# Row one-hots of a graph attention pass moved from VectorE to ScalarE, with the weights' copy and the first gathers re-ordered

## Chip, cores, metric

One core of a Trainium2 chip. The metric is the device time of one execution in microseconds; lower is better. PE is TensorE, DVE VectorE, ACT ScalarE, POOL GpSimd, SP the engine that issues most DMAs.

## What is computed

The reference is one layer of a graph network on 6250 nodes of 256 features and 100,000 edges sorted by destination. Three branches act on the normalised nodes, and the part that matters here is the first:

```python
q = (x @ Wq + bq).reshape(N, H, C)          # H = 4 heads, C = 64
k = (x @ Wk + bk).reshape(N, H, C)
v = (x @ Wv + bv).reshape(N, H, C)
alpha = jnp.sum(q[dst] * k[src], axis=-1) / jnp.sqrt(C)
amax = jax.ops.segment_max(alpha, dst, num_segments=N)
a = jnp.exp(alpha - amax[dst])
denom = jax.ops.segment_sum(a, dst, num_segments=N) + 1e-16
wv = jax.ops.segment_sum(a[:, :, None] * v[src], dst, num_segments=N)
out = wv / denom[:, :, None]
```

The second branch is linear attention with a dense block of two layers (768 hidden, gelu). A mixture of eight experts of three 256x256 layers follows on the sum.

## The kernel before

The kernel has three long stages: preparation and projections (to about 470 us), the edge pass with the dense block woven into it (to about 1860 us), and the experts.

**The edge pass.** Edges are laid out in 208 half groups (`NHF`) of four slots (`HG`) of 128 edges, each slot belonging to one window of 128 nodes. All engines run the same sequence of steps i = 0, 1, ..., each in its own instruction order, tied by semaphores; `c` is i modulo 24.

- POOL gathers the k and v rows of a half group with four indirect DMAs into one of 12 places of `ring` (`gather`, L777). From half group 12 on it waits until the place is free.
- SP loads the edges' row numbers, broadcast to all partitions, into one of four `relq` tiles (`relq_load`, L487), four half groups ahead, once `ohT_made` says that the tile was used.
- DVE makes the row one-hots `ohT` of half group i+1 (`row_one_hots`, L1652), multiplies k by the spread q (`products`, L1658), sums into `alpha` (`scores`, L1664), in `weigh` (L1711) scales v of half group i-7 (`LAG` is 7) by its attention weights, and in `add_up` (L1725, or L1720 to L1723) adds bank 0 of half group i-8 to its nodes.
- PE spreads q to edges with the one-hots (`spread_q` of half group i+2, L1210; one PSUM tile, so it needs `prod_made` of i+1), and sums v into nodes (`gather_up` of i-7, L1221), which counts `agg_ps`. Before `gather_up` PE waits for `acc_made` and `acc_copied` of i-8.
- ACT makes the one-hots for the sums in place of k (`sum_keys` of i-7: four Abs L876 and a Relu L879) and copies the other three banks of half group i-8 to the nodes (`new_windows`, L885, when `agg_ps` allows).

Every fourth step belongs to a chunk of four half groups (`CH`): a maximum over segments in steps with c % 4 = 0 (DVE L1674, L1675, then PE L1250), carries in steps with c % 4 = 1 (DVE L1681 to L1693, then PE L1256), differences with c % 4 = 2 (DVE L1699 to L1702, exponentials on ACT L905 and L907, then PE L1262 and L1263), and with c % 4 = 3 ACT copies the weights from PSUM into the ring (L898, counts `a_made`).

**The dense block** runs beside it, in turns of eight steps: `dense(c, m)` gives a turn g (0 to 24, 256 nodes in each) and a phase p = (c - 3) % 8. PE's part of a phase comes first in its step, DVE's and ACT's last. Phase 0 is the product with `w_qf` (L1166) and the start of a layer norm (DVE L1621 to L1629, ACT's square root L858), phase 1 its end (DVE), phase 2 a transpose (PE L1172, ACT L862), phases 3 to 5 the first dense layer (PE L1181, two gelus each on ACT, L868), phases 4 to 7 the second (PE L1188), and phase 7 the next turn's transpose (L1155, L853). PE's phase 4 begins with the first layer's second third, which re-uses the PSUM bank of the first:

```python
                if p in FC1:
                    pe.wait_ge(sem("fc_in"), 32)
                    pe.wait_ge(sem("m_hT_sb"), g + 1)
                    if p > 3:
                        pe.wait_ge(sem("gelu"), g * NM + 2 * (p - 3))
```

So steps with c % 4 = 2 are those of phases 3 and 7, and c % 4 = 0 those of phases 1 and 5.

## Time and profile before

| | |
|---|---|
| runs of the kernel | median 2830.92 us of 3 (2825.30 to 2831.41) |
| the profiled execution | 2825.32 us, its span 2823.6 us |
| busy share of the span | PE 89%, PE's weight loads 77%, DVE 79%, ACT 54%, POOL 33% |
| from 1000 to 1100 us, a stretch of the edge pass | PE 89.39, DVE 92.03, ACT 60.50, POOL 65.33 us busy; granted TensorE clock 0.98; DMA share 0.67 |
| chain that ended last | PE 55%, DVE 18%, issue 6%, ACT 2% |

The span is what the profile covers; the 1.7 us around it belong to the execution. The share of busy time is an average, so the stretch of the edge pass is read by itself. In rows of waits and timelines, `<-` names what ended an engine's idle time.

### The profile page before, as it was taken

The numbers are of one execution on the slowest core, as the hardware profiler recorded it, in microseconds if no ns is written. First come the engines' busy times: TensorE is split into PE (matmuls) and PEld (weight loads), VectorE is DVE, ScalarE is ACT, GpSimd is POOL, SyncE is SP. The second block draws the span as 40 slices with busy tenths as digits, with TensorE's granted clock in tenths as the row PEclk, the third lists the DMA queues.
The fourth block names the chain that finished last, engine by engine and source line by source line (L and its number), as shares of the span: only waits on it lengthen the run. The fifth ranks groups of instructions, "written<-read, shape, count | busy, mean of one in ns | idle before, by whom it ended". The sixth has DMA issues, their size and how long they took to land.

```text
span 2823.6 us, 50437 instructions
## 1 busy us (share of the span) xinstructions
PE 2508.7 (89%) x15651; PEld 2177.1 (77%) x15651; DVE 2236.2 (79%) x4398; ACT 1532.6 (54%) x3157; POOL 939.5 (33%) x891
## 2 busy tenths in 40 slices
PE   4388996899898898998998998759999999999999
PEld 2266774677777777777776776549999999999998
DVE  8797554899999999999999999756677777666775
ACT  0411110465665656655665656556666666666665
POOL 0330003666666666666666666300000000000000
PEclk9699998899999999999999999869999999999999
DMA  5210445766666666666666666510000000000000
GB/s 166 79 46 21 147 137 186 214 201 202 199 196 204 195 200 205 193 198 201 200 198 195 204 202 196 153 43 16 11 11 15 15 15 15 15 15 11 11 14 10
DMA packets 189958, 335.56 MB, mean 119 GB/s; under 512 B 31456, under 2 KB 129008, under 8 KB 189766
## 3 DMA queue, kind: packets, MB, share of 16 engines
q0 software_dynamic: 67104, 219.09, 25.9%
q1 hardware_dynamic: 116378, 108.11, 12.6%
q10 hardware_dynamic: 6316, 6.40, 0.8%
q8 instruction: 80, 1.31, 0.2%
q14 instruction: 80, 0.66, 0.1%
HBM read 293.81 MB, written 40.48 MB: 118 GB/s over the span
## 4 chain that ended last, share of the span: by engine, by line
PE 55%; DVE 18%; issue 6%; ACT 2%; DVEq 1%; DMA 1%; ACTq 0%; SPq 0%
PE ps L1324 16%; PE ps L1221 9%; PE ps L1210 8%; PE ps L1334 8%; PE ps L1188 4%; DVE ring L1658 3%; PE ps L1181 3%; DVE ring L1711 2%; PE ps L1166 2%; ACT f_more L953 1%; DVE f_split L1842 1%; DVE nodes L1725 1%; PE ps L1306 1%; DMA relq<-rel_rows 1%; DVE f_more L1858 1%
## 5 line engine op out<-in xcount | busy, mean ns | idle before, releaser
L777 POOL DMA_INDIRECT ring<-kv_rows,idx x832 | 887.4, 1067 | 738.9 <-DMA idx<-src_cols 294.8
L1324 PE MATMUL ps<-f_split,e_up 128*128 128x256 f32 (+1 forms) x3200 | 595.6, 286 | 3.5 <-DVEq L1872 1.3
L953 ACT ACTIVATE f_more<-ps,e_rest 128x256 f32<-128x256 f32 (+1 forms) x800 | 402.2, 553 | 277.7 <-PE ps L1324 276.6
L1324 PEld LDWEIGHTS ps<-f_split,e_up 128*128 128x128 f32 x3200 | 498.3, 192 | 17.4 <-issue 8.0
L1210 PE MATMUL ps<-nodes,ohT 128*128 x1664 | 413.8, 393 | 63.2 <-DVE ring L1658 56.9
L1842 DVE TENSOR_TENSOR f_split<-f_more,f_split 128x512 fp32r<-128x512 f32 (+1 forms) x400 | 272.8, 682 | 229.0 <-ACT f_split L958 222.1
L1324 PE MATMUL ps<-f_split,e_low 128*128 128x256 f32 (+1 forms) x1600 | 453.0, 283 | 0.0
L1221 PE MATMUL ps<-ring 128*128 128x260 f32 x1664 | 447.3, 415 | 0.0
L1210 PEld LDWEIGHTS ps<-nodes,ohT 128*128 128x128 f32 x1664 | 319.8, 196 | 133.0 <-issue 86.9
L1221 PEld LDWEIGHTS ps<-ring 128*128 128x128 f32 x1664 | 317.7, 201 | 43.6
L885 ACT ACTIVATE nodes<-ps 128x780 f32 x208 | 170.9, 822 | 270.3 <-PE ps L1221 249.8
L1324 PEld LDWEIGHTS ps<-f_split,e_low 128*128 128x128 f32 x1600 | 307.2, 192 | 0.0
L1334 PE MATMUL ps<-e_up,f_split 128*128 128x256 f32 x1568 | 291.3, 283 | 0.9 <-DVE f_split L1842 0.9
L876 ACT ACTIVATE ring<-iota_f,relC 128x128 f32<-128x128 f32 x832 | 263.8, 392 | 0.0
L1664 DVE TENSOR_REDUCE alpha<-ring 128x16 f32<-128x1024 f32 x208 | 254.0, 1221 | 7.1
L1711 DVE TENSOR_TENSOR ring<-ring 128x1024 f32<-128x1024 f32 x208 | 252.4, 1213 | 8.6 <-ACT ring L898 8.5
L1658 DVE TENSOR_TENSOR ring<-ring,ps 128x1024 f32<-128x1024 f32 x208 | 252.4, 1214 | 7.3 <-PE ps L1210 5.7
L1334 PEld LDWEIGHTS ps<-e_up,f_split 128*128 128x128 f32 x1568 | 244.5, 192 | 1.1 <-DVE f_split L1842 1.1
L1334 PE MATMUL ps<-e_low,f_split 128*128 128x256 f32 x784 | 221.6, 283 | 0.0
L1410 DVE TENSOR_TENSOR rows<-work,rows 128x1024 bf16<-128x1024 bf16 x196 | 159.6, 889 | 18.8 <-PE ps L1006 17.6
L1858 DVE SCALAR_TENSOR_TENSOR f_more<-ps,small,f_more 128x256 f32<-128x256 f32 x392 | 170.9, 477 | 0.7 <-PE ps L1334 0.7
L1334 PEld LDWEIGHTS ps<-e_low,f_split 128*128 128x128 f32 x784 | 150.5, 192 | 0.0
(314 smaller groups left out, 3556.2 us busy)
## 6 DMA issues: line engine op xcount, KB each, us to landing
relq<-rel_rows SPq DMA_DIRECT2D x208, 128.0 KB, 4.2
ring<-kv_rows,idx POOLq DMA_INDIRECT x832, 4.3
kv_rows<-work SPq DMA_DIRECT2D x49, 256.0 KB, 2.0
xn_rows<-nodes SPq DMA_DIRECT2D x1, 6272.0 KB, 20.4
sx_rows<-work SPq DMA_DIRECT2D x49, 128.0 KB, 1.8
nodes<-in_x_dram ACTq DMA_DIRECT2D x4, 1536.0 KB
work<-in_x_dram SPq DMA_DIRECT2D x48, 128.0 KB, 2.1
m_xn<-xn_rows SPq DMA_DIRECT2D x24, 256.0 KB, 4.3
```

The source lines that it names most:

```text
L777: pool.indirect_dma_start(out=kvh(c)[:, g, 0:2 * D], out_offset=None, in_=kvD, in_offset=bass.IndirectOffsetOnAxis(ap=idx[c // KP][:, s:s ...
L876: ins = act.activation(kv[:, g, 0:P], iota_f[:, :], ACT.Abs, bias=relC[:, ds(j * HG + g, 1)], scale=-1.0)
L953: ins = act.activation(f_whole[l][:, m * T2 * P:m * T2 * P + n * P], bank(2 * l + e % 2, m * T2 * P, m * T2 * P + n * P), ACT.Relu, bias=e ...
L1210: last = pe.matmul(ps[:, 2048 + D * g:2048 + D * (g + 1)], ohT[c % 2][:, g * P:(g + 1) * P], nodes[:, ds(win[g] * AC + HG * AC, D)], start ...
L1221: last = pe.matmul(to, kvh(cj)[:, g, 0:P], kvh(cj)[:, g, D:SL], start=(g == 0), stop=False, skip_group_check=True)
L1324: last = pe.matmul(bank(2 * l + e % 2, m * T2 * P, m * T2 * P + n * P), e_parts[l][w][:, e, i, m * P:(m + 1) * P], src_[a][:, i * T2 * P:i ...
L1334: last = pe.matmul(bank(4 + e % 2, t * D, (t + 1) * D), f_h[1][e % 2][a][:, i * T2 * P + t * P:i * T2 * P + (t + 1) * P], e_parts[2][w][:, ...
L1658: dve.tensor_tensor(k, k, ps[:, 2048:3072].rearrange("p (g d) -> p g d", g=HG), ALU.mult).then_inc(sem("prod_made"), 1)
L1664: dve.tensor_reduce(alpha[c // CH % 2][:, :].rearrange("p (h s) -> p s h", h=H)[:, c % CH * HG:(c % CH + 1) * HG, :], kvh(c)[:, :, 0:D].re ...
L1711: dve.tensor_tensor(v4, v4, kv[:, :, 2 * D:SL].unsqueeze(3).broadcast_to([P, HG, H, C]), ALU.mult).then_inc(sem("oh2_made"), 1)
L1842: dve.tensor_tensor(lo, whole, up.bitcast(F32), ALU.subtract).then_inc(sem(("h1_lo", "h2_lo")[l]), 1)
L1858: ins = dve.scalar_tensor_tensor(out=yt, in0=bank(4 + e % 2, t * D, (t + 1) * D), scalar=f_w[b][:, t * NE + e:t * NE + e + 1], in1=yt, op0 ...
```

## The change

1. The row one-hots leave DVE. ACT makes them two half groups ahead, as an Abs of (row number's difference to the partition) and a Relu of one minus it, into one of three `ohT` tiles in place of two. SP loads the first four `relq` tiles earlier, ahead of the projections' stores.
2. In ACT's step the order changes: `new_windows` and the exponentials come first, then the row one-hots, then `sum_keys`, now of half group i-6 (it waits for `alpha_made`), then, at the end of the chunk's third step (c % 4 = 2) in place of the next step, the copy of the chunk's weights, then the dense phase.
3. POOL's gathers of half groups 5 to 11 wait for the products of the half group four earlier.

```diff
--- before.py
+++ after.py
@@ -68,6 +68,7 @@
     CS = CH * HG
     NCH = NHF // CH
     LAG = 7
+    AHEAD = 4
     SHIFT = 3
     U = 2 * KP
     TURNS = NHF // U
@@ -215,7 +216,7 @@
         pen = [mid(f"pen{b}", [CS * H, P + 8], F32) for b in range(2)]
         mid("gap3", [P, AN - 2 * MH - MH // P * D - 4 * W4 - NM * TG * P - 2 * (KP * HG + CS * H + P + 8)], F32)
         ring = mid("ring", [P, RING], F32)
-        ohT = [mid(f"ohT{b}", [P, HG * P], F32) for b in range(2)]
+        ohT = [mid(f"ohT{b}", [P, HG * P], F32) for b in range(3)]
         relq = [mid(f"relq{b}", [P, HG * P], BF16) for b in range(4)]
         segF = mid("segF", [CS * H, P], F32)
         segB = mid("segB", [CS * H, P], F32)
@@ -460,6 +461,12 @@
             sp.wait_ge(sem("rows_out"), 48)
             sp.wait_ge(sem("pen_out"), 16)
 
+            def relq_load(i, c):
+                sp.dma_start(relq[c % 4][:, :], relD[ds(i * HG, HG), :].rearrange("(a g) e -> a (g e)", a=1).partition_broadcast(P)).then_inc(sem(f"relq_in{c % 4}"), 16)
+            sp.wait_ge(sem("tables_made"), 6)
+            for i in range(4):
+                relq_load(i, i)
+
             sp.sem_inc(sem("stored"), CREDIT)
 
             def store(t, k):
@@ -483,9 +490,6 @@
                 sp.dma_start(a_row[NF * i:NF * i + n, :], w.rearrange("(k p) -> k p", p=P)).then_inc(sem("mix_in"), 16)
 
 
-            def relq_load(i, c):
-                sp.dma_start(relq[c % 4][:, :], relD[ds(i * HG, HG), :].rearrange("(a g) e -> a (g e)", a=1).partition_broadcast(P)).then_inc(sem(f"relq_in{c % 4}"), 16)
-
             def chunk_load(k, b):
                 for h in range(H):
                     sp.dma_start(pen[b][h * CS:(h + 1) * CS, 0:P + 1], penD[ds(k * CS, CS), :]).then_inc(sem(f"chunk_in{b}"), 16)
@@ -510,8 +514,6 @@
             idx_load(0, 0)
             idx_load(1, 1)
             sp.wait_ge(sem("att_sb"), 8)
-            for i in range(4):
-                relq_load(i, i)
             mix_load(m_xn, xnD, 0, TG, "m_xn_in")
             mix_load(m_sx, sxD, 0, TG, "m_sx_in")
             sp.dma_start(w_f1[:, :, :], w_fc1.rearrange("(k p) n -> p k n", p=P)).then_inc(sem("fc_in"), 16)
@@ -771,6 +773,8 @@
                     pool.wait_ge(sem("att_sb"), 8)
                 if not isinstance(i, int) or i >= KP:
                     pool.wait_ge(sem("agg_ps"), i - (KP - 1))
+                elif i > AHEAD:
+                    pool.wait_ge(sem("prod_made"), i - AHEAD)
                 pool.sem_inc(sem("begun"), 1)
                 for g in range(HG):
                     s = c % KP * HG + g
@@ -872,12 +876,22 @@
 
             def sum_keys(j, cj):
                 kv = kvh(cj)
+                act.wait_ge(sem("alpha_made"), j + 1)
                 for g in range(HG):
                     ins = act.activation(kv[:, g, 0:P], iota_f[:, :], ACT.Abs, bias=relC[:, ds(j * HG + g, 1)], scale=-1.0)
                 ins.then_inc(sem("far_made"), 1)
                 act.wait_ge(sem("far_made"), j + 1)
                 act.activation(kv[:, :, 0:P], kv[:, :, 0:P], ACT.Relu, bias=1.0, scale=-1.0).then_inc(sem("sum_keys"), 1)
 
+            def row_one_hots(i):
+                t = ohT[i % 3][:, :]
+                act.wait_ge(sem(f"relq_in{i % 4}"), i // 4 * 16 + 16)
+                if i >= 3:
+                    act.wait_ge(sem("qg_ps"), i - 2)
+                act.activation(t, relq[i % 4][:, :], ACT.Abs, bias=iota_p[:, 0:1], scale=-1.0).then_inc(sem("rows_far"), 1)
+                act.wait_ge(sem("rows_far"), i + 1)
+                act.activation(t, t, ACT.Relu, bias=1.0, scale=-1.0).then_inc(sem("ohT_made"), 1)
+
             def new_windows(j):
 
                 _, base = nc.values_load_multi_w_load_instructions(base_w[0:1, ds(j, 1)], engines=(act.engine,), min_val=0, max_val=NW - 1)
@@ -887,16 +901,6 @@
 
             def step(i, c, m):
                 known = isinstance(i, int)
-                if not known or 0 <= i - LAG < NHF:
-                    sum_keys(i - LAG, (c - LAG) % U)
-                if c % CH == 3 and (not known or i >= 7 and i - 7 < NHF):
-                    kk = m * (U // CH) + (c - 7) // CH
-                    act.wait_ge(sem("ex_T"), kk + 1)
-                    if not known or i > LAG:
-                        act.wait_ge(sem("agg_ps"), i - LAG)
-                    s0 = (c - 7) % KP * HG
-                    act.activation(ring[:, s0 * SL:(s0 + CS) * SL].rearrange("p (s a) -> p s a", a=SL)[:, :, 2 * D:SL],
-                                   PS_EX.rearrange("p (h s) -> p s h", h=H), ACT.Copy).then_inc(sem("a_made"), 1)
                 if not known or i >= LAG + 1:
                     new_windows(i - (LAG + 1))
                 if c % CH == 2 and (not known or i >= 6 and i - 6 < NHF):
@@ -905,12 +909,26 @@
                     act.activation(open_m[:, 0:H], open_m[:, 0:H], ACT.Exp).then_inc(sem("open_ex"), 1)
                     act.wait_ge(sem("diff_made"), kk + 1)
                     act.activation(segD[:, :], segD[:, :], ACT.Exp).then_inc(sem("ex_made"), 1)
+                if i + 2 < NHF:
+                    row_one_hots(i + 2)
+                if 0 <= i - (LAG - 1) < NHF:
+                    sum_keys(i - (LAG - 1), (c - LAG + 1) % U)
+                if c % CH == 2 and (not known or i >= 6 and i - 6 < NHF):
+                    kk = m * (U // CH) + (c - 6) // CH
+                    act.wait_ge(sem("ex_T"), kk + 1)
+                    if not known or i >= LAG:
+                        act.wait_ge(sem("agg_ps"), i + 1 - LAG)
+                    s0 = (c - 6) % KP * HG
+                    act.activation(ring[:, s0 * SL:(s0 + CS) * SL].rearrange("p (s a) -> p s a", a=SL)[:, :, 2 * D:SL],
+                                   PS_EX.rearrange("p (h s) -> p s h", h=H), ACT.Copy).then_inc(sem("a_made"), 1)
                 g, p = dense(c, m)
                 if not known or 0 <= g < NG:
                     mix(g, p, TG, 1 if known and g == NG - 1 else TG)
                 elif g == NG:
                     mix(g, p, 1, 0)
             act.wait_ge(sem("acc_zero"), 1)
+            for i in range(2):
+                row_one_hots(i)
             mix_turned(0, TG)
             for i in range(LAST):
                 step(i, i % U, i // U)
@@ -1207,7 +1225,7 @@
                 if not isinstance(i, int) or i >= 1:
                     pe.wait_ge(sem("prod_made"), i)
                 for g in range(HG):
-                    last = pe.matmul(ps[:, 2048 + D * g:2048 + D * (g + 1)], ohT[c % 2][:, g * P:(g + 1) * P], nodes[:, ds(win[g] * AC + HG * AC, D)], start=True, stop=True)
+                    last = pe.matmul(ps[:, 2048 + D * g:2048 + D * (g + 1)], ohT[i % 3][:, g * P:(g + 1) * P], nodes[:, ds(win[g] * AC + HG * AC, D)], start=True, stop=True)
                 last.then_inc(sem("qg_ps"), 1)
 
             def gather_up(j, cj, place, width):
@@ -1645,12 +1663,6 @@
                 dve.wait_ge(sem("fc2_ps"), g + 1)
                 dve.tensor_tensor(m_sx[:, 0:n * D], bank(7, 0, n * D), m_sx[:, 0:n * D], ALU.add).then_inc(sem("m_out"), 1)
 
-            def row_one_hots(i, c, m):
-                dve.wait_ge(sem(f"relq_in{c % 4}"), m * (U // 4 * 16) + (c // 4 * 16 + 16))
-                if not isinstance(i, int) or i >= 2:
-                    dve.wait_ge(sem("qg_ps"), i - 1)
-                dve.tensor_scalar(ohT[c % 2][:, :], relq[c % 4][:, :], iota_p[:, 0:1], None, ALU.is_equal).then_inc(sem("ohT_made"), 1)
-
             def products(i, c, m):
                 dve.wait_ge(sem(f"kv_in{c % KP}"), kv_seen(c, m))
                 dve.wait_ge(sem("qg_ps"), i + 1)
@@ -1727,8 +1739,6 @@
             def step(i, c, m):
                 known = isinstance(i, int)
                 k = lambda d: m * (U // CH) + (c - d) // CH
-                if not known or i + 1 < NHF:
-                    row_one_hots(i + 1, (c + 1) % U, m + (c + 1) // U)
                 if not known or i < NHF:
                     products(i, c, m)
                     scores(i, c, k(0))
@@ -1759,7 +1769,6 @@
                 elif g == NG:
                     mix(g, p, 1)
             dve.wait_ge(sem("acc_zero"), 4)
-            row_one_hots(0, 0, 0)
             for i in range(LAST):
                 step(i, i % U, i // U)
             dve.wait_ge(sem("acc_made"), NHF)
```

## Rows read from the trace of the kernel before

**Rows 1.** Page, part 5: costliest groups, the gathers.
```profile
L777 POOL DMA_INDIRECT ring<-kv_rows,idx x832 | 887.4, 1067 | 738.9 <-DMA idx<-src_cols 294.8
```

**Rows 2.** Windows: start:end, length, busy us of PE, PEld, DVE, ACT, POOL, granted clock, DMA share, GB/s.
```profile
1040.90:1068.00 27.10, 27.10 (x144) 22.92 (x143) 23.98 (x42) 15.94 (x34) 18.36 (x18) 1.00 0.67 194
1023.80:1027.70 3.90, 3.84 (x16) 3.03 (x17) 3.87 (x6) 0.00 (x0) 0.01 (x1) 0.57 0.52 165
```

**Rows 3.** Waits from 800 to 1600 us: total, times, longest.
```profile
PE ps L1210 <- DVE ring L1658: 28.8, 16, 1.8
```

**Rows 4.** Timeline, PE, in two turns: start, length.
```profile
1010.33 2.00 PE L1221 MATMUL ps<-ring 128*128 128x260 f32 x8
...
1019.61 1.99 PE L1210 MATMUL ps<-nodes,ohT 128*128 x8 [1.80 <-DVE ring L1658]
1023.86 0.37 PE L1250 MATMUL ps<-ident,segF 64*1 64x64 f32 x2 [2.26 <-DVE segB L1675]
...
1024.48 3.33 PE L1221 MATMUL ps<-ring 128*128 128x260 f32 x8
...
1030.21 0.36 PE L1256 MATMUL ps<-ones_row,row_box 1*64 1x1 f32 x4 [0.23 <-DVE row_box L1687]
...
1036.64 0.35 PE L1262 MATMUL ps<-row_box,ones_row 1*128 1x4 f32 x2 [0.34 <-DVE nodes L1725]
...
1037.22 2.00 PE L1221 MATMUL ps<-ring 128*128 128x260 f32 x8
...
1040.91 1.89 PE L1181 MATMUL ps<-m_T,w_f 128*128 128x256 f32 x8
...
1071.83 1.99 PE L1210 MATMUL ps<-nodes,ohT 128*128 x8 [1.80 <-DVE ring L1658]
...
1092.88 1.89 PE L1181 MATMUL ps<-m_T,w_f 128*128 128x256 f32 x8
```

**Rows 5.** Timeline, DVE, in the first of them.
```profile
1015.82 0.69 DVE L1621 TENSOR_TENSOR m_x<-ps,b_qf 128x512 f32<-128x512 f32 x1 [1.23 <-PE ps L1166]
...
1018.14 1.21 DVE L1658 TENSOR_TENSOR ring<-ring,ps 128x1024 f32<-128x1024 f32 x1
...
1024.35 0.48 DVE L1652 TENSOR_SCALAR ohT<-relq,iota_p 128x512 f32<-128x512 bf16 x1
1024.75 1.21 DVE L1658 TENSOR_TENSOR ring<-ring,ps 128x1024 f32<-128x1024 f32 x1
...
1030.37 0.70 DVE L1652 TENSOR_SCALAR ohT<-relq,iota_p 128x512 f32<-128x512 bf16 x1
1031.10 1.22 DVE L1658 TENSOR_TENSOR ring<-ring,ps 128x1024 f32<-128x1024 f32 x1
```

**Rows 6.** Timeline, ACT, in the same turn.
```profile
1012.43 0.22 ACT L898 ACTIVATE ring<-ps 128x64 f32<-128x64 f32 x1 [0.17 <-PE ps L1221]
...
1033.72 1.28 ACT L905 ACT_TABLE_LOAD   x1
...
1035.43 1.28 ACT L868 ACT_TABLE_LOAD   x1
1036.73 0.84 ACT L868 ACTIVATE m_gT<-ps,m_col 128x256 f32<-128x256 f32 x2
```

**Rows 7.** Groups by form, DVE, from 474 to 1862 us.
```profile
L1652 DVE TENSOR_SCALAR ohT<-relq,iota_p 128x512 f32<-128x512 bf16 x208 | 102.2, 491 | 9.5 <-DMA relq<-rel_rows 7.7
```

**Rows 8.** Groups by form, ACT, from 474 to 1862 us.
```profile
L876 ACT ACTIVATE ring<-iota_f,relC 128x128 f32<-128x128 f32 x832 | 263.8, 392 | 0.0
...
L879 ACT ACTIVATE ring<-ring 128x512 f32<-128x512 f32 x208 | 131.3, 631 | 6.6
```

**Rows 9.** Timeline, DVE, start of the edge pass.
```profile
490.59 0.53 DVE L1652 TENSOR_SCALAR ohT<-relq,iota_p 128x512 f32<-128x512 bf16 x1 [2.88 <-DMA relq<-rel_rows]
```

**Rows 10.** Timeline, POOL, start of the edge pass.
```profile
482.88 0.95 POOL L777 DMA_INDIRECT ring<-kv_rows,idx  x1 [0.31 <-issue]
```

**Rows 11.** DMA issues, 440 to 520 us, the gathers.
```profile
ring<-kv_rows,idx POOLq DMA_INDIRECT x44, 4.7
```

## Prediction

> **What bounds the kernel now.** I began with the busy shares. In the edge pass DVE is busy for 92 us in 100 and PE for 89, ACT for 61. That invites the sum "208 one-hots off DVE", so I asked next who waits for whom. PE's longest waits on DVE come once in a turn of eight steps: 16 waits of 1.8 us in 800 us [rows 3]. I therefore laid one whole turn out in time. PE waits 1.80 us for `products` of the phase 1 step, 2.26 us for its segment maximum, 0.23 us for the carries of phase 2 and 0.34 us for `add_up` of phase 3 [rows 4]. From then on PE is busy for 27.10 of 27.10 us at full clock [rows 2]: phases 4 to 7 and 0 are bound by PE, phases 1 to 3 by DVE. The turn repeats after 1071.83 - 1019.61 = 52.2 us [rows 4]. So the change is to be priced along this alternating path, not by DVE's share.
>
> I measure from T, the start of `products` in the phase 1 step (1018.14 [rows 5]). Marks on the path are: the sums' matmuls of phase 3 at 1037.22, T + 19.08, and the start of phase 4 on PE at 1040.91, T + 22.77 [rows 4]. The next turn has T = 1070.36 (its spread starts 1.47 us behind T, as here) and phase 4 at 1092.88, T + 22.52 [rows 4].
>
> **DVE's part, phases 1 to 3.** A one-hot takes 491 ns [rows 7], but overlaps what follows: 0.40 us from its start to that of `products` in one step (1024.35 to 1024.75), 0.73 in a slow one (1030.37 to 1031.10) [rows 5]. The maximum of phase 1 stands behind no one-hot of its own step, so its sums stay at T + 6.34 (1024.48 [rows 4]). Without the one-hot `products` of phase 2 starts at T + 6.21. PE's carry matmuls came 5.46 us behind `products` (1030.21 - 1024.75 [rows 4, 5]), so now at T + 11.67. `Products` of phase 3 comes 5.62 us behind those of phase 2 (1030.37 - 1024.75), at T + 11.83, and PE's L1262 5.54 behind that (1036.64 - 1031.10), at T + 17.37; the sums 0.58 later at T + 17.95. PE itself gets there at about the same time. That is 1.13 us earlier than T + 19.08. With the old 3.69 us from these sums to phase 4 (1040.91 - 1037.22 [rows 4]), PE would begin phase 4 at T + 21.64.
>
> **ACT's part, which takes it back.** ACT's added work is an Abs and a Relu of 512 elements per step. The Relu's like takes 631 ns; the Abs has a bias pointer like L876, 392 ns at 128 elements [rows 8]. For the Abs at 512 I bound 0.6 to 0.8 us and take 0.7, so the pair is about 1.3 us. The trace of before has no such pair. On average this fits: 60.5 + 1.3 x 15.4 steps = 81 us in 100. But the order matters in the phase 3 step. Before, ACT loaded the gelu table straight after the exponentials (1035.43) and had the gelus going at 1036.73, before PE had even started its sums [rows 6]. Now windows, exponentials, one-hots, `sum_keys` and then the weights' copy stand ahead, and the copy waits for `agg_ps` of this same step's sums. The copy began 2.10 us behind the start of the sums (1012.43 [rows 6] against 1010.33 [rows 4]) and took 0.22. Then comes the table load, 1.30 us (1035.43 to 1036.73), then two gelus of 0.84 [rows 6], and 0.15 us until PE sees them: 4.63 us with two gaps of 0.02 in it. PE's phase 4 begins with a wait for exactly these two gelus. So it starts at T + 17.95 + 4.63 = T + 22.58, not at T + 21.64. Before it was T + 22.77 and T + 22.52, 22.65 in the mean: 0.07 us are gained, where 1.13 had been freed. A second limit lies close. Ahead of the copy ACT now has the windows, about 0.8 us, the exponentials with their load, 1.71 (from 1033.72 to the next load at 1035.43 [rows 6]), the one-hots, 1.3, and `sum_keys`: four Abs and a Relu are at most 4 x 0.39 + 0.63 = 2.2 us [rows 8], less their overlap about 1.9. That is 5.7 us. It starts when the sums of phase 2 are done; they begin some 0.4 us behind the carries' matmuls, at T + 12.05, and are seen 2.1 later, so at T + 14.15, and up to half a us later in turns where the sums of phase 1 ran slowly. So ACT comes to the copy between T + 19.9 and 20.4, and the sums allow it at T + 20.05. I charge 0.15 us a turn.
>
> Here the Trainium skill (ScalarE: Activation LUTs, What ACT_TABLE_LOAD costs) gives 1283 ns for a load and 1380 ns more for a drain. The trace shows the next activation 0.02 us behind the load and the load 0.02 behind the exponential [rows 6], so I add no drain; with it the gelus would come 1.38 us later still.
>
> **PE's part, phases 4 to 0.** These 29 us are PE's own and stay. At their end the layer norm of phase 0 waits for PE (1.23 us at 1015.82 [rows 5]) and the one-hot behind it on DVE is on the path: 0.40 us gained per turn. The new copy comes no later for `weigh` than the old, since both waited for the same `agg_ps`. The one-hots for `spread_q` are ready 2.1 + 0.8 + 1.3 = 4.2 us behind the start of the previous sums; in between PE has those sums, a spread, mostly a dense product, and the next sums, each of 1.8 to 2.0 us [rows 4], so it doesn't wait for them. Where an exponential's 1.71 us comes ahead they are ready after 5.9 us, and those steps have the dense product.
>
> **Sum of a turn:** 0.40 + 0.07 - 0.15 = 0.32 us, in 24 full turns 7.7 us.
>
> **Start.** DVE waited 2.88 us for `relq` at 490.59 and made the fourth product at 491.05 [rows 9]. Now `relq` is there early, and the gathers decide: the last of half group 3 is issued from 482.88 to 483.83 [rows 10] and a gather lands after 4.7 us [rows 11], at 488.5. That is 2.5 us, with 0 and 5 as bounds. POOL issues a half group in 5.0 us and one gather takes 1067 ns in the mean [rows 1], so half group i begins 5 us behind i-1 anyway; the product of i-4 is then done, and the new wait holds back next to nothing. SP's four early `relq` loads now stand ahead of its projection stores, where DVE and PE have yet to make the first tile, and no longer ahead of the dense block's first loads; I count neither (bounds 0 and 2 us). **End.** The last steps behind the dense turns are DVE's, and there each one-hot counts: six by 0.42 us, 2.5 us; bounds 0 and 8 x 0.49.
>
> **Total:** 7.7 + 2.5 + 2.5 = 12.7 us. Against the profiled execution, 2825.3 us, that is 2812.6. That execution is as fast as the fastest run, the median is 2830.9, so the median to expect is 2818 (-0.45%). About 0.2%, 5.6 us, is what can be told from no change.
>
> **Rivals.**
> - *The freed time stays.* If the gelus are not late, PE begins phase 4 at T + 21.64: 22.58 + 0.15 - 21.64 = 1.09 us more per turn, 26 us more, 2792. For it: ACT idles often. Against it: the wait in the code and 4.63 > 3.69. 0.16.
> - *DVE was the bound throughout.* 208 x 0.46 = 96 us, 2735. Against it: 27 us of unbroken PE work in each turn. 0.04.
> - *No change that can be measured.* The ACT chain is 0.3 us longer (Abs at 0.8, a later copy), or the start gives nothing: 2825 to 2837. 0.18.
> - *Slower, by the clock.* PE had 1.80 and 2.26 us of waits near each other, and behind them it ran at a granted 0.57, between 1.2 and 2.4 GHz; the sums took 3.33 us in place of 2.00 [rows 2, 4]. The new wait of phase 4, about 1 us, makes a third gap, at the head of the stretch in which every slow matmul counts. If each turn lost 1.33 us there, that is 32 us and the time 2850; it becomes slower than before by 0.2% when over half of the turns do. Against it: the next turn had the same two waits and its sums did not lag (phase 4 at T + 22.52). 0.17.
> - *A rule says otherwise.* Simple functions would be dearer on ACT than they free on DVE: the chain is then decided by ACT in more steps than phase 3. By rows, 1.3 us for 0.49 removed; if one more phase of each turn waited by that difference, 0.8 us, the turn would lose 0.5, 12 us, and the median be 2838. On average ACT has 19 us in 100 left, so 0.03. The Trainium skill (ScalarE: Activation LUTs, Rules for kernel authors) states it: relu, min and max belong on VectorE, not on ScalarE.
>
> My forecast holds 0.42, itself 2808 to 2825. The range must reach to the first rival and toward the clock's: 2786 to 2842. Faster by over 0.2% is the forecast (0.41 of it), the first two rivals and the better edge of "no change": 0.62. Within 0.2%: 0.18. Slower: 0.20.
>
> **What the new profile would show.** DVE's share in the edge pass falls from 92 to about 85 us in 100 and ACT's rises to about 81. PE waits once a turn, about 1 us, before L1181 of phase 4, for ACT's gelu; the wait for `products` is still there near 1.8 us. From T to phase 4 stays 22.6 us, a turn takes 51.9 us. Wrong would be: no wait for the gelus (first rival), slow sums behind it (the clock), or an Abs far from 0.7 us.

## The result and the profile after

| | before | after |
|---|---|---|
| median | 2831.41 us of 9 runs (2825.30 to 2837.96) | 2824.02 us of 9 runs (2821.73 to 2831.82) |
| ratio | | 0.9977, 95% interval 0.9967 to 0.9988 |
| the profiled execution | 2825.32 us | 2824.02 us, its span 2822.3 us |

The change makes the kernel 7.4 us faster, 0.23%, where 12.7 us (0.45%) had been forecast: the sign was right, the size wrong. A second set of runs, below, has 4.0 us.

The page (part 1) and the windows of the changed kernel (columns as in [rows 2]):
```profile
PE 2509.7 (89%) x15651; PEld 2180.3 (77%) x15651; DVE 2160.4 (77%) x4190; ACT 1775.7 (63%) x3573; POOL 932.0 (33%) x891
...
1000.00:1100.00 100.00, 87.69 (x461) 72.48 (x460) 87.19 (x155) 78.53 (x161) 67.58 (x63) 1.00 0.65 200
```
In a stretch of the edge pass DVE went from 92.03 to 87.19 us in 100, ACT from 60.50 to 78.53. PE, which has the same work as before, is busy for 87.69 us in place of 89.39. Part of the difference is that the stretch before holds sums that ran slowly (3.33 us in place of 2.00 [rows 4]) and the stretch after holds none; its granted clock is 1.00, before it was 0.98. PE thus still waits, no less than before. For what, the waits of the changed kernel from 800 to 1600 us tell (as [rows 3]):
```profile
PE ps L1268 <- DVE segB L1687: 34.7, 15, 2.6
PE ps L1228 <- DVE ring L1670: 22.0, 16, 1.4
DVE m_x L1639 <- PE ps L1184: 21.2, 16, 1.3
...
PE ps L1199 <- ACT m_gT L872: 13.3, 15, 0.9
```
The wait for `products` (L1228) fell from 1.8 to 1.4 us a turn, since no one-hot stands ahead of them behind the layer norm. A new wait of 0.89 us once a turn has come: PE's first product of phase 4 (L1199) waits for ACT's gelus (L872).

PE in one turn and the marks of the next, in the timeline of the changed kernel (as [rows 4]):
```profile
1025.13 1.99 PE L1228 MATMUL ps<-nodes,ohT 128*128 x8 [1.37 <-DVE ring L1670]
1029.42 0.27 PE L1268 MATMUL ps<-ident,segF 64*1 64x64 f32 x2 [2.30 <-DVE segB L1687]
...
1035.47 0.36 PE L1274 MATMUL ps<-ones_row,row_box 1*64 1x1 f32 x4 [1.49 <-DVE row_box L1699]
1035.76 0.23 PE L1234 MATMUL ps<-zeros 128*128 128x4 bf16 x3
1035.85 2.00 PE L1239 MATMUL ps<-ring 128*128 128x260 f32 x8
1037.69 1.89 PE L1228 MATMUL ps<-nodes,ohT 128*128 x8
1039.42 1.89 PE L1199 MATMUL ps<-m_T,w_f 128*128 128x256 f32 x8
1041.25 0.37 PE L1280 MATMUL ps<-row_box,ones_row 1*128 1x4 f32 x2
...
1041.84 2.00 PE L1239 MATMUL ps<-ring 128*128 128x260 f32 x8
1043.68 1.89 PE L1228 MATMUL ps<-nodes,ohT 128*128 x8
1046.45 1.97 PE L1199 MATMUL ps<-m_T,w_f 128*128 128x256 f32 x8 [0.89 <-ACT m_gT L872]
...
1077.03 1.99 PE L1228 MATMUL ps<-nodes,ohT 128*128 x8 [1.37 <-DVE ring L1670]
...
1093.95 2.00 PE L1239 MATMUL ps<-ring 128*128 128x260 f32 x8
...
1098.56 1.97 PE L1199 MATMUL ps<-m_T,w_f 128*128 128x256 f32 x8 [0.89 <-ACT m_gT L872]
```
ACT in the phase 3 step of that turn (as [rows 6]):
```profile
1037.99 0.82 ACT L899 ACTIVATE nodes<-ps 128x780 f32 x1 [1.20 <-PE ps L1239]
1038.83 1.28 ACT L909 ACT_TABLE_LOAD   x1
1040.12 0.20 ACT L909 ACTIVATE row_box<-row_box 1x4 f32<-1x4 f32 x1
1040.23 0.29 ACT L911 ACTIVATE segD<-segD 64x128 f32<-64x128 f32 x1
1040.43 0.70 ACT L891 ACTIVATE ohT<-relq,iota_p 128x512 f32<-128x512 bf16 x1
1041.17 0.63 ACT L893 ACTIVATE ohT<-ohT 128x512 f32<-128x512 f32 x1
1041.71 1.26 ACT L881 ACTIVATE ring<-iota_f,relC 128x128 f32<-128x128 f32 x4
1043.00 0.63 ACT L884 ACTIVATE ring<-ring 128x512 f32<-128x512 f32 x1
1043.94 0.22 ACT L922 ACTIVATE ring<-ps 128x64 f32<-128x64 f32 x1 [0.30 <-PE ps L1239]
1044.18 1.28 ACT L872 ACT_TABLE_LOAD   x1
1045.47 0.84 ACT L872 ACTIVATE m_gT<-ps,m_col 128x256 f32<-128x256 f32 x2
```
The copy (L922) waits for the sums' matmuls that began at 1041.84, and the table load and the gelus stand behind it. From the sums to phase 4 are 1046.45 - 1041.84 = 4.61 us (second turn 4.61), where 3.69 had been in the first turn of [rows 4].

`Products` of DVE in the same turn (as [rows 5]), with the layer norm's end (L1652) and `add_up` (L1737); the first is T:
```profile
1023.65 1.22 DVE L1670 TENSOR_TENSOR ring<-ring,ps 128x1024 f32<-128x1024 f32 x1
...
1029.26 0.84 DVE L1652 TENSOR_SCALAR m_xn<-m_x,m_mv,m_rs 128x256 f32<-128x256 f32 x2
1030.02 1.21 DVE L1670 TENSOR_TENSOR ring<-ring,ps 128x1024 f32<-128x1024 f32 x1
...
1035.71 1.22 DVE L1670 TENSOR_TENSOR ring<-ring,ps 128x1024 f32<-128x1024 f32 x1
...
1040.63 0.47 DVE L1737 SCALAR_TENSOR_TENSOR nodes<-nodes,follows,ps 128x260 f32 x1
```

**Where the 7.4 us lie.** Each trace was cut at the same marks: POOL's first gather, PE's phase 0 products, ACT's last windows. All figures are differences of starts in PE's, ACT's and POOL's timelines, in us; a turn is the mean of 23.

```text
kernel          first gather   gather to   first   mean    last phase 0   first gather
                starts at      phase 0     turn    turn    to windows     to last windows
before          463.85         32.23       49.67   52.01   114.38         1392.5
before, again   472.47         32.06       49.42   51.99   111.44         1388.6
after           474.43         29.19       48.38   51.97   107.98         1380.7
after, again    472.36         29.28       50.27   51.99   110.40         1385.6
```
Means of the pairs: start -2.9, first turn -0.2, 23 turns of -0.02 each -0.5, end -3.7; together -7.4, as much as the medians differ by. That the two agree so well is partly luck: two profiles of one kernel are 3.9 and 4.9 us apart in this span. The preparation scatters by 8.6 us in one and the same kernel, and the profiled execution of before had a short one. Turns are measured to a few hundredths, the end only to some 2 us.

### The profile page after: what moved, and what is told of

Its sections match the earlier page's. It is cut to its first block, busy times and chain, and to the rows that moved or that the text cites. A ratio compares the mean times of both kernels' runs of the same rounds, so it can differ in the third digit from the quotient of the medians.

```text
span 2822.3 us, 50644 instructions
## 1 busy us (share of the span) xinstructions
PE 2509.7 (89%) x15651; PEld 2180.3 (77%) x15651; DVE 2160.4 (77%) x4190; ACT 1775.7 (63%) x3573; POOL 932.0 (33%) x891
## 4 chain that ended last, share of the span: by engine, by line
PE 69%; DVE 17%; issue 6%; ACT 4%; DVEq 1%; DMA 1%; ACTq 0%; SPq 0%; POOL 0%; POOLq 0%
PE ps L1342 16%; PE ps L1239 12%; PE ps L1228 9%; PE ps L1352 8%; PE ps L1199 5%; PE ps L1105 5%; PE ps L1206 4%; DVE rows L1428 3%; DVE ring L1670 2%; DVE ring L1723 2%; PE ps L1184 2%; ACT f_more L971 1%; DVE f_split L1851 1%; PE ps L1234 1%; PE ps L1324 1%
## 5 line engine op out<-in xcount | busy, mean ns | idle before, releaser
L1228 PE MATMUL ps<-nodes,ohT 128*128 x1664 | 408.9, 390 | 45.7 <-DVE ring L1670 43.7
L1239 PE MATMUL ps<-ring 128*128 128x260 f32 x1664 | 441.0, 411 | 0.0
L1228 PEld LDWEIGHTS ps<-nodes,ohT 128*128 128x128 f32 x1664 | 323.0, 196 | 105.3 <-issue 58.7
L1723 DVE TENSOR_TENSOR ring<-ring 128x1024 f32<-128x1024 f32 x208 | 254.0, 1221 | 12.7 <-ACT ring L922 12.1
L1428 DVE TENSOR_TENSOR rows<-work,rows 128x1024 bf16<-128x1024 bf16 x196 | 159.9, 899 | 20.1 <-PE ps L1024 18.7
L1199 PE MATMUL ps<-m_T,w_f 128*128 128x256 f32 (+1 forms) x600 | 141.1, 378 | 23.0 <-ACT m_gT L872 23.0
```

The costliest lines, as they stand in the source:

```text
L1199: last = pe.matmul(bank(6, f % 2 * TG * P, f % 2 * TG * P + n * P), w_f1[:, i, f * P:(f + 1) * P], m_T[:, i * TG * P:i * TG * P + n * P], ...
L1228: last = pe.matmul(ps[:, 2048 + D * g:2048 + D * (g + 1)], ohT[i % 3][:, g * P:(g + 1) * P], nodes[:, ds(win[g] * AC + HG * AC, D)], start ...
L1239: last = pe.matmul(to, kvh(cj)[:, g, 0:P], kvh(cj)[:, g, D:SL], start=(g == 0), stop=False, skip_group_check=True)
L1723: dve.tensor_tensor(v4, v4, kv[:, :, 2 * D:SL].unsqueeze(3).broadcast_to([P, HG, H, C]), ALU.mult).then_inc(sem("oh2_made"), 1)
```

## The experiments

My theory: the time from T to phase 4 is given back through the new wait, because ACT's weights' copy waits for this step's sums and the gelus stand behind it; moved, about 1.1 us a turn comes free. The rivals: DVE's one-hots free nothing on the path anyway; ACT's added work or the clock takes it back.

**Both kernels again**, to see what their profiles agree in.

> The kernel before, profiled once more, as a measure of how much stages scatter from one execution to the next. If the preparation stage (up to the first gather, 463.85 us before and 474.43 us after) scatters by some us by itself, this execution shows it off 463.85 by several us, and the 10.6 us by which the changed kernel's profile came later to its first gather are chance. If they belong to the change, this one is near 464. The edge pass from first gather to the last copy of sums should be 1392.5 us again within 2, a turn 52.0 us.

> The changed kernel once more. Theory: ratio 0.9977 again (within 0.996 to 0.999), first gather anywhere from 464 to 475 us, edge pass from first gather to last copy of sums 1380.8 us within 2, a turn 51.97 us. Rival (the early row loads make the preparation longer): first gather again near 474.

The profiled execution of before took 2830.06 us, beside a median of 2830.20 in 17 other runs of it; after 2826.18 (2822.74 to 2830.64), ratio 0.9987 (0.9978 to 0.9997). This set puts the change at 4.0 us (0.13%), where the result above has 7.4 (0.23%): it is clear that the changed kernel is faster, but not by how many microseconds.

The mean turn is the same again, 51.99 and 51.99. The span from the first gather to the last windows came out at 1388.6 and 1385.6 us, 4 and 5 us from the first profiles, so the expected "within 2" was missed in both kernels. The first gather of before stands at 472.47 this time, so the preparation does scatter by itself. In the profiles that follow (without those of one slower chip, see below) it stands at 467.6 to 472.5 with the early `relq` loads and at 472.3 and 472.7 without them, which shows no cost of these loads.

**The copy alone.** In the kernel before only the copy moves, from the next step to behind the exponentials of the third step, ahead of the dense phase.

```diff
-                if c % CH == 3 and (not known or i >= 7 and i - 7 < NHF):
-                    ... (the weights' copy, ahead of new_windows)
                 new_windows(i - (LAG + 1))
...
                     act.activation(segD[:, :], segD[:, :], ACT.Exp).then_inc(sem("ex_made"), 1)
+                if c % CH == 2 and (not known or i >= 6 and i - 6 < NHF):
+                    ... (the weights' copy, with agg_ps i + 1 - LAG)
                 g, p = dense(c, m)
```


> The kernel before with only one part of the change: the copy of the chunk's weights at the end of the chunk's third step, ahead of that step's dense phase. One-hots stay on DVE, all else as before. My theory: with the sums of phase 3 at T + 19.1 the gelus end 4.6 us later, at T + 23.7, where PE had begun phase 4 at T + 22.65 in the mean; a turn costs 1.0 us more (53.0 us), the whole 20 to 25 us more than before. Rival (the gelus have slack on PE): within 3 us of before.

Measured 2853.89 us (2849.07 to 2859.66), ratio 1.0080 (1.0065 to 1.0095), 23.7 us slower than before as expected, a turn 52.98. ACT in its timeline, phase 3 step:
```profile
999.86 1.28 ACT L897 ACT_TABLE_LOAD   x1
...
1005.37 0.22 ACT L906 ACTIVATE ring<-ps 128x64 f32<-128x64 f32 x1 [3.81 <-PE ps L1221]
1005.61 1.28 ACT L868 ACT_TABLE_LOAD   x1
1006.91 0.84 ACT L868 ACTIVATE m_gT<-ps,m_col 128x256 f32<-128x256 f32 x2
```
and PE in that step:
```profile
1003.28 2.00 PE L1221 MATMUL ps<-ring 128*128 128x260 f32 x8
...
1007.89 1.97 PE L1181 MATMUL ps<-m_T,w_f 128*128 128x256 f32 x8 [0.77 <-ACT m_gT L868]
```
ACT sits idle for 3.81 us in front of the copy and the table load behind it can't begin. Sums to phase 4: 4.61 us, as in the changed kernel, without a single one-hot on ACT. This part of the change costs 0.99 us a turn by itself.

**The one-hots without the copy.** In the changed kernel the copy goes back to the start of the next step. The rest of the change stays: the one-hots on ACT, the other order of ACT's step, the early loads and POOL's wait.

```diff
             def step(i, c, m):
+                if c % CH == 3 and (not known or i >= 7 and i - 7 < NHF):
+                    ... (the weights' copy, with agg_ps i - LAG)
                 new_windows(i - (LAG + 1))
...
                     sum_keys(i - (LAG - 1), (c - LAG + 1) % U)
-                if c % CH == 2 and (not known or i >= 6 and i - 6 < NHF):
-                    ... (the weights' copy)
```


> The changed kernel with the weights' copy back in the next step, there first in ACT's order: the one-hots move to ACT, the copy's move is undone. Theory: the gelus no longer wait for this step's sums, only for `sum_keys`; a turn of 51.4 to 51.5 us as with the gelus ahead of the copy, 12 us less than the changed kernel. Rival (ACT is too full and only the load of work counts): 52.0.

> The changed kernel with the weights' copy back in the next step, again. Theory: turns of 51.4 to 51.5 us, ratio near 0.9945, as the PE's wait for gelus is then set by `sum_keys` ahead of them. Rival: 52.0 and 0.998.

This kernel and the three below with two expectations were measured on two chips, one after the other. On the first, with the kernel before at 2909.21 us, it took 2885.13, a ratio of 0.9922 (0.9902 to 0.9943); on the second, with the kernel before at 2829.69, 2814.10 (2811.13 to 2817.79), ratio 0.9942 (0.9921 to 0.9963), a turn 51.41, as expected. On the first chip `products` waited very long in single places, in one kernel 17.8 and 20.1 us at the start, when the spreads that they need had been done. That leaves the gathers, but these traces hold no landing times of them, so this is inferred. Turns scattered from 51.5 to 58.6 us there, so ratios of the first chip are told but its turns not read.

The wait before phase 4 is down to 0.39 us in the mean of 23 turns and not gone: ACT still has one-hots and `sum_keys` ahead of the gelus.

**The copy behind the gelus.** In the changed kernel's phase 3 step alone the copy moves behind the dense phase.

```diff
-                if c % CH == 2 and (not known or i >= 6 and i - 6 < NHF):
+                if c % 8 == 2 and (not known or i >= 6 and i - 6 < NHF):
                     ... (the weights' copy)
                 g, p = dense(c, m)
                 ... (mix)
+                if c % 8 == 6 and (not known or i >= 6 and i - 6 < NHF):
+                    ... (the weights' copy)
```


> The changed kernel with one order altered: in the steps of phase 3 ACT copies the chunk's weights behind the two gelus, not ahead of them. My theory (the gelus stand behind a copy that waits for this step's sums, and hold PE 4.6 us behind the start of those sums): the wait of PE before L1199 of phase 4, 0.89 us, falls below 0.5 us, a turn gets 0.5 to 0.8 us shorter, 51.3 us, and the time 12 to 19 us shorter than the changed kernel's, 2808 at a median of 2824. Rival one (ACT as a whole is too full, the copy is not what holds it): the gelus come as late as before, a turn stays at 52.0. Rival two (phases 1 to 3 give the time back somewhere else, on DVE or PE): the wait for the gelu goes, but the turn stays at 52.0.

Measured 2813.77 us (2809.25 to 2820.18), ratio 0.9945 (0.9932 to 0.9959), a turn 51.45, the wait again 0.39 us. That is 12.4 us less than the changed kernel, the low end of what was expected. `weigh` on DVE now waits for the later copy, 26.5 us in 15 waits from 800 to 1600 us; the turn shortens nonetheless.

**The gelus ahead of `sum_keys` too.** In the phase 3 step ACT's order becomes windows, exponentials, one-hots, dense phase, copy, `sum_keys`.

```diff
                     row_one_hots(i + 2)
+                if c % 8 == 6:
+                    ... (dense and mix, then the weights' copy, then sum_keys)
+                else:
                     ... (sum_keys, the weights' copy, dense and mix, as before)
```


> The changed kernel with ACT's order in phase 3 steps altered: windows, exponentials, row one-hots, then the gelus, then the weights' copy, and `sum_keys` last. Theory: the gelus end about 24.2 us behind the turn's start (phase 0 on PE), before PE is free for phase 4 at 25.6 us; PE's wait for them (0.9 us in the changed kernel, some 0.5 with the gelus right behind `sum_keys`) is gone, and DVE's `weigh`, which waited up to 2 us for the late copy there, does not wait. A turn of 50.9 to 51.1 us, 22 to 26 us less than the changed kernel, about 2800. Rival (what is left of the time is set by another wait that opens when this one goes, `sum_keys` for the sums of phase 4): a turn of 51.3 to 51.5 us, no better than with the gelus ahead of the copy alone (51.45).

> Gelus ahead of copy and `sum_keys` in phase 3, again, since the last execution's gathers landed late and its turns scattered from 51.5 to 58.6 us. Theory as then: turns of 50.9 to 51.1 us where gathers are in time, PE not waiting for gelus, ratio 0.991 to 0.993. Rival: a new wait takes it, turns of 51.3 to 51.5 us and a ratio near 0.9945, as with the gelus ahead of the copy alone.

On the first chip 2895.00 us, ratio 0.9955 (0.9937 to 0.9974); on the second, with the kernel before at 2829.69, 2797.91 (2797.81 to 2798.14), ratio 0.9881 (0.9863 to 0.9898), a turn 50.85. The turn is at the edge of the expectation (50.9 to 51.1), and the second ratio is better than the expected 0.991 to 0.993. PE in its timeline on the second chip, phase 3 into 4:
```profile
1027.45 0.38 PE L1297 MATMUL ps<-row_box,ones_row 1*128 1x4 f32 x2
...
1028.06 2.00 PE L1256 MATMUL ps<-ring 128*128 128x260 f32 x8
1029.89 1.89 PE L1245 MATMUL ps<-nodes,ohT 128*128 x8
1031.62 1.89 PE L1216 MATMUL ps<-m_T,w_f 128*128 128x256 f32 x8
```
and ACT there:
```profile
1027.39 0.63 ACT L893 ACTIVATE ohT<-ohT 128x512 f32<-128x512 f32 x1
1028.03 1.28 ACT L872 ACT_TABLE_LOAD   x1
1029.33 0.84 ACT L872 ACTIVATE m_gT<-ps,m_col 128x256 f32<-128x256 f32 x2
1030.15 0.22 ACT L926 ACTIVATE ring<-ps 128x64 f32<-128x64 f32 x1
```
The gelus start 1.27 us behind the sums (1029.33 - 1028.06) in place of 3.63, PE goes from sums to phase 4 in 3.56 us with no wait, and the copy comes without a wait too, at 1030.15, since its sums are done by then. On the second chip this is the fastest version of all, by 31.8 us against the kernel before. Against the mean of the two profiles of before its profile has 26.5 us less in 23 turns, 3.0 in the first turn, 2.2 at the start and 1.5 at the end, together 33.2, within the scatter of such spans. On the first chip it came behind the one-hots without the copy (2895.00 against 2885.13 us), so it isn't shown to be the best where `products` wait that long.

The mean start on PE of each mark behind phase 0's product, 23 turns of each kernel, in us:

```text
                       before  before,  after  after,  copy   one-hots  copy     gelus
                               again           again   alone  alone     behind   ahead of
                                                                        gelus    sum_keys
spread behind products  5.72   5.72     5.29   5.29    5.71   5.29      5.29     5.29
carries                16.32  16.31    15.68  15.70   16.31  15.65     15.67    15.70
sums of phase 3        23.15  23.14    22.07  22.08   23.09  22.03     22.07    22.09
phase 4                26.81  26.79    26.69  26.71   27.71  26.14     26.18    25.65
next phase 0           52.01  51.99    51.97  51.99   52.98  51.41     51.45    50.85
```
Down to the sums every kernel with one-hots on ACT is equally far ahead (1.05 to 1.12 us). What the kernels keep of it is decided between the sums and phase 4, but for 0.08 us behind it. The parts don't add up: without the copy's move the one-hots give 0.58 us a turn, the copy alone costs 0.99, and both together give 0.02. With the copy ahead of the gelus phase 4 comes 4.6 us behind the sums whatever ACT has to do besides, so there the one-hots save 1.01 us (52.98 to 51.97). Without it the one-hots and `sum_keys` themselves hold the gelus up, and 0.58 is left.

**The start.** First the early `relq` loads go back to their old place; then POOL's new wait is dropped.

```diff
-            sp.wait_ge(sem("tables_made"), 6)
-            for i in range(4):
-                relq_load(i, i)
             sp.sem_inc(sem("stored"), CREDIT)
...
             sp.wait_ge(sem("att_sb"), 8)
+            for i in range(4):
+                relq_load(i, i)
```


> The changed kernel with the first four row loads back in their old place, behind the attention part. Theory (the early loads are what shortens the start): from the first gather to the first dense product of phase 0 it is 31 to 33 us again (32.3 and 32.0 before, 29.2 changed). Rival (the rest of the change does it): 29 us. Turns 52.0 in both.

> The changed kernel with the first four row loads at their old place, again. Theory: 31 to 33 us from the first gather to the first dense product of phase 0 (29.2 in both profiles of the changed kernel, 32.3 and 32.0 before). Rival: 29 us. Turns 52.0.

A single run on each chip: 2913.22 and 2836.10 us. From the first gather to phase 0 it takes 34.2 us in the second, against 29.2; 31 to 33 had been expected. PE in its timeline:
```profile
496.63 1.99 PE L1226 MATMUL ps<-nodes,ohT 128*128 x8 [1.58 <-DVE ring L1668]
503.26 3.77 PE L1226 MATMUL ps<-nodes,ohT 128*128 x8 [4.64 <-ACT ohT L891]
506.83 3.11 PE L1182 MATMUL ps<-w_qf,m_T 128*128 128x256 f32 x8
```
The spread of the fifth half group waits 4.64 us for its one-hots, and these for the fifth `relq` load: ACT makes them at 501.73, after 9.86 us of waiting for that transfer. That is 29.1 us behind the first gather; in the two profiles of the changed kernel it is 22.5 and 20.8. SP issues the fifth load only once ACT has used the first tile, which itself arrives late here.

```diff
-                elif i > AHEAD:
-                    pool.wait_ge(sem("prod_made"), i - AHEAD)
```


> The changed kernel without POOL's waits for products at half groups 5 to 11. Theory: nothing changes that an execution can show; first gather to first phase 0 product 29.2 us, the next one 48 to 50 us later, turns 52.0. Rival (the waits keep the DMA engines free for the row loads): the start gets longer by 1 to 3 us.

> The changed kernel without POOL's waits at half groups 5 to 11, again. Theory: first gather to first phase 0 product 29.2 us within 0.5, turns 52.0. Rival: 1 to 3 us longer at the start.

2915.09 and 2823.58 us, a single run each. In the second phase 0 starts 28.2 us behind the first gather, 1.1 earlier than with the wait, and a turn takes 51.98. The products of half groups 0 to 2 start 10.4, 15.8 and 21.1 us behind it (with the wait 10.3, 15.9 and 20.6), those of half group 3 24.9 against 25.9. Between the last two lies one spread, of 1.99 us here and 3.67 there. The second profile of the changed kernel, which has the wait, settles it: its spread takes 1.99 us too, and the products of half group 3 start 24.9 us behind the first gather. POOL issues at the same 5.0 us per half group in all three. So the wait holds nothing back that these profiles show.

## Why the prediction was right or wrong

**What fails is one step: from T to the sums of phase 3, "T + 17.95", 1.13 us earlier than before.** In the profile after the sums stand at 1041.84 - 1023.65 = T + 18.19, and at T + 18.40 in the next turn. On the average of 23 turns, T being 1.47 us before the spread, the sums moved from 23.14 - 4.25 = T + 18.89 to 22.08 - 3.82 = T + 18.26. So 0.63 us were freed where the forecast has 1.13. The missing half has two parts.

- 0.19 us had never been there. T + 19.08 was read from one turn, and in that trace the 23 turns run from T + 18.82 to T + 19.12.
- 0.31 us are lost on the way, most of it on DVE ahead of phase 3. `Products` of phase 3 start at 1035.71, T + 12.06 (12.09 in the mean), where T + 11.83 was forecast; those of phase 2 at T + 6.37, not 6.21. Most of this 0.16 is the layer norm's end on DVE, which takes 0.84 us (1029.26) and took 0.73 before (the first row below). In the mean of 23 turns it is 0.82 in both profiles of the changed kernel and in those of the one-hots without the copy and of the gelus first, and 0.73 in both profiles of before and in the copy alone's. So it comes with the one-hots on ACT. Why it takes longer is not shown.

```profile
1023.70 0.73 DVE L1634 TENSOR_SCALAR m_xn<-m_x,m_mv,m_rs 128x256 f32<-128x256 f32 x2
...
1036.02 0.47 DVE L1725 SCALAR_TENSOR_TENSOR nodes<-nodes,follows,ps 128x260 f32 x1
```
From there on the forecast's chain held: 5.54 us behind these `products` is T + 17.60, and L1280 on PE starts at 1041.25, just there. It follows `add_up` by 0.62 us (1040.63 to 1041.25), as before (1036.02 to 1036.64, where the trace names `add_up` as what PE waited for). The forecast said of PE's own chain that it "gets there at about the same time", without a price. From the carries at 1035.47 to the sums PE is indeed busy back to back, for 6.37 us; behind the forecast's own carries at T + 11.67 that would have been T + 18.04. The chains end within about 0.1 us of each other: L1280 keeps the 0.62 us behind `add_up` (0.61 to 0.63) in 18 of 23 turns, and in five, at 0.73 to 0.77, PE comes last.

**The half that takes it back was right to 0.02 us.** Sums to gelus to PE: 4.63 forecast, 4.61 measured in the timelines of the changed kernel and of the copy alone. With the sums late, all that had been freed and more went: T to phase 4 was 22.55 in the mean before (the forecast had 22.65, from two turns) and is 26.70 - 3.82 = 22.88. Forecast was a gain of 0.07 less a charge of 0.15, so a loss of 0.08; measured is a loss of 0.33. The charge itself (ACT coming to the copy later than the sums allow) wasn't needed: ACT waited 0.30 us there. By luck it stood in for half of the step that was missed.

**The one-hot behind the layer norm** was to give 0.40 us a turn and gives 0.43 (5.72 to 5.29).

**Phases 4 to 0** were to stay; they became 0.08 longer (25.20 to 25.28). The first product behind the wait takes 1.97 us for 1.89, which is that much; with the gelus first there is no wait, the product takes 1.89 and the stretch 25.20.

**Sum of a turn:** 0.43 - 0.33 - 0.08 = 0.02 us, where 0.32 was forecast. In 24 turns about 0.5 us came in place of 7.7.

**Start:** 2.5 us forecast, 2.9 measured. The forecast's mark was the fourth product, 24.7 us behind the first gather. It came 25.9 and 24.9 us behind it, after 27.2 and 28.0 before, so 2.2 us earlier in the mean; the other 0.7 lie between it and phase 0, where single spreads take from 2.0 to 3.8 us. The reading was incomplete in two ways. The gathers decide only part of the first products: in the first profile after those at 490.32 and 495.06 waited 3.11 and 2.26 us for them, but the fourth, at 500.32, waited 2.78 us for its spread. And the run with late `relq` loads shows a second effect that had been left out: the fifth tile's load is tied to the first tile's use. With the one-hots on ACT and the loads in their old place the start was 2 us longer than before, in a single run. **End:** 2.5 us forecast; 3.7 measured, with 2 to 3 us of scatter between executions of one kernel, so it isn't told from 2.5.

The measured -7.4 us is thus start and end. The forecast had put most of its gain into the turns, where there was none.

**ACT's pair** was put at 1.3 us: Abs 0.71 and Relu 0.63, from start to end 1.37 in step order, 1.28 until the next instruction begins (1040.43 to 1041.71). ACT's share was to be 81 and is 78.5; DVE's 85 and is 87.2. The wait for `products`, expected "still near 1.8 us", is 1.37: I had the 0.40 in the sum and forgot it in this sentence.

**The rivals.** *The freed time stays*: false for this kernel, borne out where the gelus are not late. It asked that the gelus not be late and put 1.09 us on that; with the gelus first a turn is 1.13 us shorter than with the change and the time 2797.91, near its 2792. *DVE as the bound throughout* is out: with all one-hots off DVE, and nothing late, a turn loses 1.15 us, not the 8 x 0.46 = 3.7 it would have been. *No change that can be measured*: it asked for a chain 0.3 us longer or a start that gives nothing. T to phase 4 came out worse by 0.25 us than forecast, though not by ACT, and start and end kept the first result just outside of its 0.2%; the second, 0.13%, lies inside. *The clock*: the new gap of 0.89 us did no such thing; the granted clock from 1000 to 1100 us is 1.00 (the level of 2.4 GHz), and the next sums behind it take 2.00 us, in each of the 23 turns of both profiles after. Slow are only the sums of phase 1, behind the two waits that were there before: over 2.1 us in 16 and 17 of 23 turns before and in 13 and 11 after. *The rule* fell as well: with the one-hots moved to ACT and the copy left where it was the kernel is faster by 0.6%, about 2 us of these 16 at the start, so here it doesn't pay to keep them on DVE, which the Trainium skill (ScalarE: Activation LUTs, Rules for kernel authors) would have advised. The same page (What ACT_TABLE_LOAD costs) has 1283 ns for a load, and the 1.28 us of the rows agree; of its 1380 ns for a drain no row shows anything, the gelu following 0.01 us behind the load (1044.18 + 1.28 to 1045.47).

Open stays what of the end's 3.7 us is the change's, and why the layer norm's end takes 0.1 us longer. The other order of ACT's step (windows first, `sum_keys` a half group earlier) was never run without the one-hots.

## What to carry to other kernels

When an instruction that waits for engine A is moved ahead of a function that A waits for, price the loop that it closes, from A's own instruction on and back to A. Here that was 4.6 us behind the sums and could be read off the old trace to 0.02 us. When a forecast is the small difference of large marks, take the marks from many turns: here one turn's T + 19.08 and two turns' 22.65 stood 0.19 and 0.10 us off their means, and the whole forecast was 0.32 us a turn. When two chains reach a mark "at about the same time", price both. And if a change frees time and moves an order at once, look for the order that keeps the time: here another order of ACT's step turned a gain of 7 us into one of 32.

## What the runs showed that was not expected

- Preparation, with unchanged code, took 463.85 us in one execution and 472.47 in another of the same kernel; a stage mark is worth more than a span where the change is 7 us.
- A time bought by moving 0.49 us off a 92% busy engine can be nil, and 1.1 us come back from an engine that is idle 21% of the time, by order alone.
- The chain through DVE and the chain through PE end within about 0.1 us of each other once the one-hots are off DVE, so by these times taking more off either alone would bring the sums forward by no more than that.
- On one chip the kernel before took 2909 us in place of 2830, and the kernels that were profiled there had single long waits of `products`, probably for gathers; the kernel before was not profiled there. The ratios kept their sign (0.9922 and 0.9955 against 0.9942 and 0.9881), but not their order, and the lead of the version with the gelus first was 0.45% in place of 1.19%.
